# Two bit-linear stages: one normalised tile of four moves to ACT, and the high part is written from unscaled data

## The chip, the cores and the metric

The program runs on one NeuronCore of a Trainium2 chip. The metric is device time of one execution in microseconds, from runs on the chip; of the kernel before there are three, and one more execution that was profiled. Engines are called by the profile's names: PE (matmul), DVE (vector), ACT (activations), POOL, and SP, which only issues transfers here. SBUF and PSUM are the core's memories, PSUM being the one that PE writes.

## The reference

The program is a chain of six residual stages over x of shape 4 x 1024 x 256 (4096 rows): a binarised feed-forward layer, local attention, the feed-forward layer again, a bit-linear layer, attention with relative positions, and the bit-linear layer again. Only the two bit-linear layers matter here. Each gets the layer-normalised x and adds half its result to x:

```
def _L1_ffn_ref(x, weight, ln_gamma, ln_beta):
    LN_EPS = 0.001; EPS = 1e-05; QB = 128.0
    mu = jnp.mean(x, axis=-1, keepdims=True)
    var = jnp.var(x, axis=-1, keepdims=True)
    xn = (x - mu) * jax.lax.rsqrt(var + LN_EPS) * ln_gamma + ln_beta
    beta = jnp.mean(jnp.abs(weight))
    w_q = jnp.clip(ste_round(weight / (beta + EPS)), -1.0, 1.0)
    gamma = jnp.max(jnp.abs(xn))
    xq = jnp.clip(xn * QB / gamma, -QB + EPS, QB - EPS)
    y = jnp.einsum('bsd,du->bsu', xq, w_q)
    return y * (gamma * beta / QB)
...
    x = x + 0.5 * _L1_ffn_ref(x, weight, gamma, beta)
```

`gamma` is one number for all 4096 x 256 values, so the largest value must be known before any row is scaled: that cuts the layer in two halves. `xq` is not rounded, so the matmul needs more than one f16 factor's precision.

## The kernel before, in words

x stays in SBUF as `G.x`, 32 tiles of 128 rows x 256 columns. Mean and variance per row are in `G.mv`, left there by the stage before. A chunk is CT = 4 tiles (512 rows); there are NC = 8 chunks. `bit_phase` is called twice, as stage 4 (`b0_` tiles, from 855 us in the profile) and as stage 6, the last (`b1_` tiles, from 2221 us, where the results are also stored). The profile shows both under `b_`.

Each engine runs its own list of instructions in order, written out by hand; semaphores (`s[...]`) order the engines among each other. A `wait_ge` holds everything behind it on its engine.

First half, per chunk i:
- DVE normalises four tiles into `xn` (line 1181), which has two buffers, so from chunk 2 on it waits for the transposes of chunk i-2. Then it takes the largest absolute value of chunk i-1 (`largest`, line 1173). After chunks 1 and 3 it also does parts of the quantisation of the weight.
- PE transposes the chunk's tiles into PSUM `psT`, in two halves k of 128 features (line 1251).
- ACT multiplies by the layer's gain and adds its offset, PSUM to `xT` in SBUF (line 1129), once for each k.

Then DVE and POOL find the global maximum, and DVE writes `gi` (128 over the maximum, line 1195).

Second half, per chunk i:
- ACT scales `xT` in place by `gi` (line 1134), DVE clips it in place (`clip`, line 1199), ACT copies it to f16 as `xhi` (line 1139), DVE writes the f16 rest as `xlo` (`low_part`, line 1206).
- PE multiplies both parts by the ternary weight, 16 matmuls into `psY` (line 1262), and raises `Y`.
- DVE adds the result times `osc` to x (`residual`, line 1212). In stage 4 it also takes the moments for the next stage (lines 1220 and 1226); in stage 6 SP stores the chunk.

`xhi`, `xlo` and `psY` have two buffers each: the high and low parts of chunk i wait for `Y` of chunk i-2. ACT's list is scale 0, scale 1, high 0, scale 2, high 1, scale 3, (wait for Y 0) high 2, and so on. DVE's list is clip 0, clip 1, low 0, clip 2, low 1, residual 0, clip 3, low 2, residual 1, and so on, with aggregate and moments beside the residual in stage 4.

Of the kernel before, what the change touches and what calls it, by code (L numbers as in the profile page):

```python
# [7 lines left out]
ALU = mybir.AluOpType  # L8
ACT = mybir.ActivationFunctionType
AX = mybir.AxisListType  # L10
P = 128
B, S, D = 4, 1024, 256
NT = B * S // P
TPB = S // P
KD = D // P
HID = 1024
MH = HID // P
CT = 4
NC = NT // CT
# [13 lines left out]
def step(eng, ins, c):  # L33

    ins.then_inc(c.sem, 1)
    c.k += 1
    eng.wait_ge(c.sem, c.value())


def sems(nc, G, prefix, names):  # L40

    s = {n: nc.alloc_semaphore(f"{prefix}_{n}") for n in names.split()}
    G.live.extend(s.values())
    return s
# [1014 lines left out]
def bit_phase(nc, G, A, r, out=None):  # L1059
# [3 lines left out]
    with ExitStack() as ctx:  # L1063
        sb = lambda n, sh, d=F32: ctx.enter_context(nc.sbuf_tensor(f"b{r}_{n}", sh, d))
# [6 lines left out]
        eps = sb("eps", [P, 2])  # L1071
        sd = sb("sd", [P, NT])
        rstd = sb("rstd", [P, NT])
        var = sb("var", [P, NT])
        sd2 = sb("sd2", [P, NT])
        scl = sb("scl", [P, NT])
        wsum = sb("wsum", [P, 1])
        wall = sb("wall", [P, 1])
        thr = sb("thr", [P, 2])
        tmax = sb("tmax", [P, NC])  # L1080
        pmax = sb("pmax", [P, 1])
        gall = sb("gall", [P, 1])
        gi = sb("gi", [P, 1])
        osc = sb("osc", [P, 1])
        xn = sb("xn", [P, 2, CT, D])
        xT = sb("xT", [P, NC, KD, CW])
        xhi = sb("xhi", [P, 2, KD, CW], F16)
# [1 line left out]
        sums = sb("sums", [P, CT, 6])  # L1089
        psT = ps("psT", [P, 2, KD, 512])  # L1090
        psY = ps("psY", [P, 2, CT, D])
        s = sems(nc, G, f"bit{r}", "w_in gb_in eps sd norm var sd2 scl wsum wall quant xn xT xTev tmax max1 gmax gdve "
                 "scaled xq xhi xlo Y out sums stat stored")
        block = ctx.enter_context(nc.Block())

        @block.sync
        def _(sp):
            with nc.allow_non_contiguous_dma("gamma and beta by feature, once"):
                sp.dma_start(gm[:, :], A["gamma"].rearrange("(k p) -> p k", p=P)).then_inc(s["gb_in"], 16)
                sp.dma_start(bt[:, :], A["beta"].rearrange("(k p) -> p k", p=P)).then_inc(s["gb_in"], 16)  # L1100
            sp.dma_start(w[:, :, :], A["weight"].rearrange("(k p) d -> p k d", p=P)).then_inc(s["w_in"], 16)
            clear_old(G, sp)
            sp.wait_ge(s["gb_in"], 32)
            if last_phase:
                rows = out.rearrange("b (t p) d -> p (b t) d", p=P)
                for i in range(NC):
                    sp.wait_ge(s["out"], i + 1)
                    sp.dma_start(rows[:, i * CT:(i + 1) * CT, :],
                                 G.x[:, i * CT:(i + 1) * CT, :]).then_inc(s["stored"], 16)
                sp.wait_ge(s["stored"], 16 * NC)  # L1110
# [8 lines left out]
        @block.scalar  # L1119
        def _(act):  # L1120
            act.wait_ge(s["eps"], 1)
            nc.scalar.activation(sd[:, :], G.mv[:, :, 1], ACT.Sqrt, bias=eps[:, 0:1]).then_inc(s["sd"], 1)  # L1122
            act.wait_ge(s["var"], 1)
            nc.scalar.activation(sd2[:, :], var[:, :], ACT.Sqrt, bias=eps[:, 1:2]).then_inc(s["sd2"], 1)  # L1124
            act.wait_ge(s["gb_in"], 32)
            for i in range(NC):
                for k in range(KD):
                    act.wait_ge(s["xT"], i * KD + k + 1)
                    nc.scalar.activation(xT[:, i, k, :], psT[:, i % 2, k, :], ACT.Identity, bias=bt[:, k:k + 1],
                                         scale=gm[:, k:k + 1]).then_inc(s["xTev"], 1)  # L1130
            act.wait_ge(s["gdve"], 4)
            for i in range(NC + 1):
                if i < NC:
                    nc.scalar.activation(xT[:, i, :, :], xT[:, i, :, :], ACT.Copy, scale=gi[:, :]).then_inc(s["scaled"], 1)  # L1134
                if i >= 1:
                    act.wait_ge(s["xq"], i)
                    if i >= 3:
                        act.wait_ge(s["Y"], i - 2)
                    nc.scalar.activation(xhi[:, (i - 1) % 2, :, :], xT[:, i - 1, :, :], ACT.Copy).then_inc(s["xhi"], 1)  # L1139

        @block.vector
        def _(dve):
# [3 lines left out]
            norm = Count(s["norm"])  # L1146
# [4 lines left out]
            scale = Count(s["scl"])  # L1151
            step(dve, nc.vector.reciprocal(scl[:, :], sd2[:, :]), scale)  # L1152
            step(dve, nc.vector.tensor_tensor(scl[:, :], scl[:, :], rstd[:, :], ALU.mult), scale)

            quant = Count(s["quant"])

            def quantise(part):
                if part == 0:
                    dve.wait_ge(s["w_in"], 16)
                    nc.vector.tensor_reduce(wsum[:, :], w[:, :, :], AX.XY, ALU.add,  # L1160
                                            apply_absolute_value=True).then_inc(s["wsum"], 1)
                if part == 1:
                    dve.wait_ge(s["wall"], 1)
                    step(dve, nc.vector.tensor_scalar(wall[:, :], wall[:, :], 1.0 / (D * D), None, ALU.mult), quant)
                    step(dve, nc.vector.tensor_scalar(thr[:, 0:1], wall[:, :], 1e-5, 0.5, ALU.add, ALU.mult), quant)
                    step(dve, nc.vector.tensor_scalar(thr[:, 1:2], thr[:, 0:1], -1.0, None, ALU.mult), quant)
                    step(dve, nc.vector.tensor_scalar(wt[:, :, :], w[:, :, :], thr[:, 1:2], None, ALU.is_lt), quant)
                    nc.vector.scalar_tensor_tensor(wq[:, :, :], w[:, :, :], thr[:, 0:1], wt[:, :, :], ALU.is_gt,
                                                   ALU.subtract).then_inc(s["quant"], 1)

            def largest(i):
                dve.wait_ge(s["xTev"], i * KD + KD)
                nc.vector.tensor_reduce(tmax[:, i:i + 1], xT[:, i, :, :], AX.XY, ALU.max,
                                        apply_absolute_value=True).then_inc(s["tmax"], 1)

            for i in range(NC):
                if i >= 2:
                    dve.wait_ge(s["xT"], (i - 1) * KD)
                for t in range(CT):
                    g = i * CT + t  # L1180
                    nc.vector.tensor_scalar(xn[:, i % 2, t, :], G.x[:, g, :], G.mv[:, g, 0:1], scl[:, g:g + 1],  # L1181
                                            ALU.subtract, ALU.mult).then_inc(s["xn"], 1)
                if i in (1, 3):
                    quantise(i // 2)
                if i >= 1:
                    largest(i - 1)
# [4 lines left out]
            g = Count(s["gdve"])  # L1191
# [8 lines left out]
                                        ALU.max).then_inc(s["xq"], 1)  # L1200

            def low_part(i):
                dve.wait_ge(s["xhi"], i + 1)
                if i >= 2:
                    dve.wait_ge(s["Y"], i - 1)
                nc.vector.tensor_tensor(xlo[:, i % 2, :, :], xT[:, i, :, :], xhi[:, i % 2, :, :],  # L1206
                                        ALU.subtract).then_inc(s["xlo"], 1)
# [35 lines left out]
        @block.tensor  # L1243
        def _(pe):
            for i in range(NC):
                pe.wait_ge(s["xn"], i * CT + CT)
                if i >= 2:
                    pe.wait_ge(s["xTev"], (i - 1) * KD)
                for k in range(KD):
                    for t in range(CT):  # L1250
                        last = nc.tensor.transpose(psT[:, i % 2, k, t * P:t * P + P], xn[:, i % 2, t, k * P:k * P + P],
                                                   G.ident[:, :])
                    last.then_inc(s["xT"], 1)
            pe.wait_ge(s["quant"], 5)
            for i in range(NC):
                pe.wait_ge(s["xlo"], i + 1)
                if i >= 2:
                    pe.wait_ge(s["out"], i - 1)
                for t in range(CT):
                    for k in range(KD):  # L1260
                        for part, x in enumerate((xhi, xlo)):
                            last = nc.tensor.matmul(psY[:, i % 2, t, :], x[:, i % 2, k, t * P:t * P + P], wq[:, k, :],  # L1262
                                                    start=(k + part == 0), stop=(k == KD - 1 and part == 1),
                                                    skip_group_check=True)
                last.then_inc(s["Y"], 1)
# [1279 lines left out]
```

## Time and profile before

| | us |
|---|---|
| median of 3 runs (lowest, highest) | 2291.6 (2290.39, 2296.07) |
| the profiled execution's own time | 2287.45 |
| its span, first to last instruction | 2285.7 |
| PE busy in the span | 2010.9 (88%) |
| DVE busy | 1642.6 (72%) |
| ACT busy | 1221.4 (53%) |
| POOL busy | 495.5 (22%) |
| TensorE clock granted, mean over the span | 0.936 |

Busy time is the time in which an engine was executing; register, branch, semaphore and transfer-issuing instructions are not counted. The shares are averages over six stages with different limits, so they say little of one stage. The clock is a share of TensorE's full 2.4 GHz; 0.50 is its other level, 1.2 GHz. Start times count from the start of the span. The last 5.6 us of the span, after the last residual, are the last store.

### The profile page before, as it was taken

The numbers are of one execution on the slowest core, as the hardware profiler recorded it, in microseconds if no ns is written. First come the engines' busy times: TensorE is split into PE (matmuls) and PEld (weight loads), VectorE is DVE, ScalarE is ACT, GpSimd is POOL, SyncE is SP. The second block draws the span as 40 slices with busy tenths as digits, with TensorE's granted clock in tenths as the row PEclk, the third lists the DMA queues.
The fourth block names the chain that finished last, engine by engine and source line by source line (L and its number), as shares of the span: only waits on it lengthen the run. The fifth ranks groups of instructions, "written<-read, shape, count | busy, mean of one in ns | idle before, by whom it ended". The sixth has DMA issues, their size and how long they took to land. (4 is left out here: it accounts for less than half of the span.)

```text
span 2285.7 us, 74481 instructions
## 1 busy us (share of the span) xinstructions
PE 2010.9 (88%) x32248; PEld 1276.1 (56%) x32248; DVE 1642.6 (72%) x2668; ACT 1221.4 (53%) x1870; POOL 495.5 (22%) x804
## 2 busy tenths in 40 slices
PE   3996999999987985798878999999999999999985
PEld 2663565656655654457854555555555555555543
DVE  6776555554546778776676888888888888888847
ACT  3772232313234765223315777777776777777754
POOL 0003000000000000000014544345443544435410
PEclk8998898999999996899967999999999999999997
DMA  3001000000000000342485544545544555455312
GB/s 113 1 1 28 21 2 20 3 20 3 1 21 1 1 1 5 103 144 97 190 294 139 144 128 129 133 127 140 132 128 127 145 142 133 115 138 138 101 29 74
DMA packets 273791, 195.11 MB, mean 85 GB/s; under 512 B 206744, under 2 KB 260310, under 8 KB 273210
## 3 DMA queue, kind: packets, MB, share of 16 engines
q1 hardware_dynamic: 262586, 139.27, 23.9%
q0 software_dynamic: 10496, 50.75, 5.9%
q8 instruction: 256, 4.19, 0.8%
q14 instruction: 69, 0.57, 0.1%
q10 hardware_dynamic: 384, 0.33, 0.0%
HBM read 91.69 MB, written 93.88 MB: 81 GB/s over the span
## 5 line engine op out<-in xcount | busy, mean ns | idle before, releaser
L2158 DVE TENSOR_REDUCE a1c_nm<-a1c_S 128x1 f32<-128x1024 f32 x512 | 609.6, 1218 | 83.6 <-PE a1c_S L2245 83.1
L2092 ACT ACTIVATE a1c_PT<-a1c_ST 128x1024 f32<-128x1024 f32 x499 | 509.8, 1022 | 67.0 <-PE a1c_ST L2245 64.3
L2109 ACT ACTIVATE a1c_Pb<-a1c_S,a1c_nm 128x192 f32<-128x192 f32 (+1 forms) x512 | 212.2, 415 | 202.5 <-DVE a1c_nm L2158 201.2
L2031 POOL TENSOR_TENSOR a1c_lt<-a1c_lt 128x256 f32<-128x256 f32 (+5 forms) x448 | 254.0, 567 | 35.5
L2148 DVE COPY a1c_PbT<-a1c_T 96x512 f32<-96x512 f32 x256 | 175.8, 687 | 98.5 <-PE a1c_T L2277 96.1
L2245 PE MATMUL a1c_ST<-a1c_Q,a1c_KR 57*128 57x256 f16 (+2 forms) x1066 | 176.5, 286 | 29.6 <-ACT a1c_PT L2092 19.3
L2245 PE MATMUL a1c_S<-a1c_KL,a1c_Q 54*32 54x512 f16 (+11 forms) x3136 | 193.7, 327 | 0.3
L2245 PE MATMUL a1c_S<-a1c_KR,a1c_Q 54*32 54x512 f16 (+13 forms) x2816 | 182.0, 317 | 12.8 <-DMA a1c_Gx<-a_bias 10.2
L2245 PE MATMUL a1c_S<-a1c_Gx,ident 64*32 64x96 f32 (+2 forms) x4352 | 186.1, 242 | 0.0
L2023 POOL DMA_DIRECT2D a_band<-a1c_Pb x128 | 71.0, 555 | 494.7 <-ACT a1c_Pb L2109 494.6
L2277 PE MATMUL a1c_T<-ident,a1c_Pb 128*96 128x128 f32 x1024 | 169.5, 289 | 0.8 <-DVE a1c_mhl L2172 0.8
L2245 PE MATMUL a1c_ST<-a1c_Q,a1c_KL 57*128 57x128 f16 (+1 forms) x932 | 150.0, 266 | 17.5 <-ACT a1c_PT L2092 16.8
L596 ACT ACTIVATE a_PT<-a_R 128x1024 f32<-128x1024 f32 x80 | 77.5, 1021 | 144.4 <-PE a_R L956 94.2
L1115 POOL PARTITION_ALL_REDUCE b_wall<-b_wsum x2 | 0.8, 404 | 704.4 <-DVE b_wsum L1160 704.4
L2277 PEld LDWEIGHTS a1c_T<-ident,a1c_Pb 128*96 128x96 f32 x1024 | 102.7, 129 | 88.8 <-issue 55.7
L312 DVE TENSOR_TENSOR f_hlo<-f_h,f_hhi 128x512 f16<-128x512 f32 x128 | 88.0, 687 | 69.1 <-ACT f_hhi L230 69.0
L2245 PEld LDWEIGHTS a1c_S<-a1c_Gx,ident 64*32 64x32 f32 x4352 | 126.4, 110 | 14.0 <-issue 0.7
L225 ACT ACTIVATE f_h<-f_psH,b,a 128x512 f32<-128x512 f32 x128 | 99.3, 776 | 59.8 <-PE f_psH L336 58.3
L2245 PE MATMUL a1c_PV<-a1c_PT,a1c_VU 128*17 128x512 f32 (+3 forms) x1280 | 127.5, 470 | 0.0
L2245 PE MATMUL a1c_PV<-a1c_PT,a1c_VL 128*17 128x512 f32 (+3 forms) x1280 | 127.4, 470 | 0.0
L655 DVE TENSOR_REDUCE a_mx<-a_R 128x8 f32<-128x1024 f32 x64 | 75.4, 1221 | 66.8 <-PE a_R L878 66.8
L347 PE MATMUL f_psY<-sw2T,f_hhi 128*128 128x256 f16 x512 | 118.6, 273 | 1.0 <-DVE f_hlo L312 1.0
(366 smaller groups left out, 4096.4 us busy)
## 6 DMA issues: line engine op xcount, KB each, us to landing
a_band<-a1c_Pb POOLq DMA_DIRECT2D x128, 384.0 KB, 3.4
a_bias<-a1b_G SPq DMA_DIRECT2D x32, 768.0 KB, 9.3
a1c_Gx<-a_bias SPq DMA_DIRECT2D x128, 192.0 KB, 4.4
a1c_Dt<-a_band SPq DMA_DIRECT2D x128, 126.0 KB, 3.7
a1c_Q<-a_qk SPq DMA_DIRECT2D x192, 64.0 KB
a1c_Vw<-a_values SPq DMA_DIRECT2D x64, 102.0 KB, 3.0
a1c_KL<-a_qk SPq DMA_DIRECT2D x96, 64.0 KB
a1c_KR<-a_qk SPq DMA_DIRECT2D x90, 64.0 KB
```

What stands on the lines that cost most here:

```text
L225: nc.scalar.activation(h[:, n % NB, :], psH[:, n % NB, :], ACT.Gelu, bias=G.b1[:, m:m + 1], scale=G.a1[:, m:m + 1]).then_inc(s["h"], 1)
L312: nc.vector.tensor_tensor(hlo[:, n % NB, :], h[:, n % NB, :], hhi[:, n % NB, :], ALU.subtract).then_inc(s["hlo"], 1)
L347: last = nc.tensor.matmul(psY[:, i % 2, t, :], x[:, n % NB, t * P:t * P + P], G.sw2T[:, m, :], start=(m + part + t % 2 == 0), stop=(m == M ...
L596: nc.scalar.activation(PT[:, n % 2, 2 * a:2 * a + 2, :], R[:, 2 * a:2 * a + 2, :], ACT.Exp, scale=0.25).then_inc(s["sexp"], 1)
L655: nc.vector.tensor_reduce(dst[:, 2 * a:2 * a + 2], src[:, 2 * a:2 * a + 2], AX.X, ALU.max, negate=True).then_inc(s["smax"], 1)
L2031: add = lambda o, x, y: nc.gpsimd.tensor_tensor(o, x, y, ALU.add)
L2092: nc.scalar.activation(PT[:, q % 8, :, :], place(q), ACT.Exp).then_inc(s["exp"], 1)
L2109: nc.scalar.activation(Pb[:, band_slot(I, c), w0:w1], SP[:, t % 2, I * P - 32 + w0:I * P - 32 + w1], ACT.Exp, bias=nm[:, t // 16 % 2, col: ...
L2148: nc.vector.tensor_copy(PbT[:, e % RING, :], T[0:BW, :]).then_inc(s["Tb_ev"], 1)
L2158: nc.vector.tensor_reduce(nm[:, t // 16 % 2, col:col + 1], SP[:, t % 2, :], AX.X, ALU.max, negate=True).then_inc(s["max"], 1)
L2245: return nc.tensor.matmul(out, w, x, start=start, stop=stop, skip_group_check=True)
L2277: ins = nc.tensor.transpose(T[0:BW, at:at + P], Pb[:, band_slot(I, c), BW * ch:BW * ch + BW], G.ident[:, :])
```

## The change

In the first half DVE normalises three tiles of a chunk and ACT the fourth, as `scl * x + off`, with a new small tile `off` = -mean * `scl` that DVE computes once per stage. ACT does this for chunk i+1 ahead of its affine instructions of chunk i. PE waits for both engines.

In the second half ACT writes `xhi` straight from the unscaled `xT` with the scale `gi`, and only then scales `xT` in place; it waits for its own high part before that. ACT's list becomes high 0, scale 0, high 1, scale 1, (wait for Y 0) high 2, scale 2, (wait for Y 1) high 3, scale 3, and so on. DVE's clip still waits for the scale and its list keeps its order; the low part now waits for the clip instead of the high part. The high part is thus that of the unclipped value, and the low part is the clipped value less it.

```diff
--- before.py
+++ after.py
@@ -1074,6 +1074,7 @@
         var = sb("var", [P, NT])
         sd2 = sb("sd2", [P, NT])
         scl = sb("scl", [P, NT])
+        off = sb("off", [P, NT])
         wsum = sb("wsum", [P, 1])
         wall = sb("wall", [P, 1])
         thr = sb("thr", [P, 2])
@@ -1089,7 +1090,7 @@
         sums = sb("sums", [P, CT, 6])
         psT = ps("psT", [P, 2, KD, 512])
         psY = ps("psY", [P, 2, CT, D])
-        s = sems(nc, G, f"bit{r}", "w_in gb_in eps sd norm var sd2 scl wsum wall quant xn xT xTev tmax max1 gmax gdve "
+        s = sems(nc, G, f"bit{r}", "w_in gb_in eps sd norm var sd2 scl wsum wall quant xn xna xT xTev tmax max1 gmax gdve "
                  "scaled xq xhi xlo Y out sums stat stored")
         block = ctx.enter_context(nc.Block())
 
@@ -1122,21 +1123,30 @@
             nc.scalar.activation(sd[:, :], G.mv[:, :, 1], ACT.Sqrt, bias=eps[:, 0:1]).then_inc(s["sd"], 1)
             act.wait_ge(s["var"], 1)
             nc.scalar.activation(sd2[:, :], var[:, :], ACT.Sqrt, bias=eps[:, 1:2]).then_inc(s["sd2"], 1)
+            def normalise(i):
+                g = i * CT + CT - 1
+                if i >= 2:
+                    act.wait_ge(s["xT"], (i - 1) * KD)
+                nc.scalar.activation(xn[:, i % 2, CT - 1, :], G.x[:, g, :], ACT.Identity, bias=off[:, g:g + 1],
+                                     scale=scl[:, g:g + 1]).then_inc(s["xna"], 1)
+
             act.wait_ge(s["gb_in"], 32)
+            act.wait_ge(s["scl"], 3)
+            normalise(0)
             for i in range(NC):
+                if i + 1 < NC:
+                    normalise(i + 1)
                 for k in range(KD):
                     act.wait_ge(s["xT"], i * KD + k + 1)
                     nc.scalar.activation(xT[:, i, k, :], psT[:, i % 2, k, :], ACT.Identity, bias=bt[:, k:k + 1],
                                          scale=gm[:, k:k + 1]).then_inc(s["xTev"], 1)
             act.wait_ge(s["gdve"], 4)
-            for i in range(NC + 1):
-                if i < NC:
-                    nc.scalar.activation(xT[:, i, :, :], xT[:, i, :, :], ACT.Copy, scale=gi[:, :]).then_inc(s["scaled"], 1)
-                if i >= 1:
-                    act.wait_ge(s["xq"], i)
-                    if i >= 3:
-                        act.wait_ge(s["Y"], i - 2)
-                    nc.scalar.activation(xhi[:, (i - 1) % 2, :, :], xT[:, i - 1, :, :], ACT.Copy).then_inc(s["xhi"], 1)
+            for i in range(NC):
+                if i >= 2:
+                    act.wait_ge(s["Y"], i - 1)
+                nc.scalar.activation(xhi[:, i % 2, :, :], xT[:, i, :, :], ACT.Copy, scale=gi[:, :]).then_inc(s["xhi"], 1)
+                act.wait_ge(s["xhi"], i + 1)
+                nc.scalar.activation(xT[:, i, :, :], xT[:, i, :, :], ACT.Copy, scale=gi[:, :]).then_inc(s["scaled"], 1)
 
         @block.vector
         def _(dve):
@@ -1151,6 +1161,7 @@
             scale = Count(s["scl"])
             step(dve, nc.vector.reciprocal(scl[:, :], sd2[:, :]), scale)
             step(dve, nc.vector.tensor_tensor(scl[:, :], scl[:, :], rstd[:, :], ALU.mult), scale)
+            step(dve, nc.vector.scalar_tensor_tensor(off[:, :], G.mv[:, :, 0], -1.0, scl[:, :], ALU.mult, ALU.mult), scale)
 
             quant = Count(s["quant"])
 
@@ -1176,7 +1187,7 @@
             for i in range(NC):
                 if i >= 2:
                     dve.wait_ge(s["xT"], (i - 1) * KD)
-                for t in range(CT):
+                for t in range(CT - 1):
                     g = i * CT + t
                     nc.vector.tensor_scalar(xn[:, i % 2, t, :], G.x[:, g, :], G.mv[:, g, 0:1], scl[:, g:g + 1],
                                             ALU.subtract, ALU.mult).then_inc(s["xn"], 1)
@@ -1200,7 +1211,7 @@
                                         ALU.max).then_inc(s["xq"], 1)
 
             def low_part(i):
-                dve.wait_ge(s["xhi"], i + 1)
+                dve.wait_ge(s["xq"], i + 1)
                 if i >= 2:
                     dve.wait_ge(s["Y"], i - 1)
                 nc.vector.tensor_tensor(xlo[:, i % 2, :, :], xT[:, i, :, :], xhi[:, i % 2, :, :],
@@ -1243,7 +1254,8 @@
         @block.tensor
         def _(pe):
             for i in range(NC):
-                pe.wait_ge(s["xn"], i * CT + CT)
+                pe.wait_ge(s["xn"], (i + 1) * (CT - 1))
+                pe.wait_ge(s["xna"], i + 1)
                 if i >= 2:
                     pe.wait_ge(s["xTev"], (i - 1) * KD)
                 for k in range(KD):
```

## Rows read from the trace of the kernel before

**Rows 1.** Last stage's second half: us; busy PE, PEld, DVE, ACT, POOL; PEclk, DMA, GB/s

```profile
2251.60:2280.20 28.60, 17.32 (x128) 13.03 (x128) 23.98 (x24) 16.65 (x16) 0.00 (x0) 0.84 0.37 125
```

**Rows 2.** Chain of waits, last stage: start us, us, what

```profile
2262.70 1.28 DVE x L1212
2263.97 0.60 DVE b_xT L1199
...
2265.63 1.28 DVE x L1212
```

**Rows 3.** Timeline of DVE, last stage's first half: start us, us, what, [idle before]

```profile
2224.68 0.19 DVE L1153 TENSOR_TENSOR b_scl<-b_scl,b_rstd 128x32 f32<-128x32 f32 x1
2224.91 2.67 DVE L1181 TENSOR_SCALAR b_xn<-x,mv,b_scl 128x256 f32<-128x256 f32 x8
...
2238.17 1.22 DVE L1173 TENSOR_REDUCE b_tmax<-b_xT 128x1 f32<-128x1024 f32 x1
...
2241.13 1.22 DVE L1173 TENSOR_REDUCE b_tmax<-b_xT 128x1 f32<-128x1024 f32 x1 [0.46 <-ACT b_xT L1129]
...
2248.92 1.22 DVE L1173 TENSOR_REDUCE b_tmax<-b_xT 128x1 f32<-128x1024 f32 x1 [1.20 <-ACT b_xT L1129]
```

**Rows 4.** Timelines of PE and ACT, last stage's first half, chunk 4

```profile
2238.31 1.97 PE L1251 MATMUL b_psT<-ident,b_xn 128*128 128x128 f32 x8 [2.20 <-DVE b_xn L1181]
...
2239.46 1.63 ACT L1129 ACTIVATE b_xT<-b_psT,b_bt,b_gm 128x512 f32<-128x512 f32 x2 [2.54 <-PE b_psT L1251]
```

**Rows 5.** ACT's groups, shapes apart: line, names, shapes, count, busy us, mean ns

```profile
L2109 ACT ACTIVATE a1c_Pb<-a1c_S,a1c_nm 128x192 f32<-128x192 f32 x384 | 161.8, 421 | 156.4 <-DVE a1c_nm L2158 155.2
...
L1134 ACT ACTIVATE b_xT<-b_xT,b_gi 128x1024 f32<-128x1024 f32 x16 | 18.0, 1134 | 5.4 <-DVE b_gi L1195 5.4
L1139 ACT ACTIVATE b_xhi<-b_xT 128x1024 f16<-128x1024 f32 x16 | 16.8, 1053 | 18.6 <-PE b_psY L1262 11.7 <-DVE b_xT L1199 6.8
```

**Rows 6.** Timeline of ACT, last stage's second half

```profile
2251.61 2.19 ACT L1134 ACTIVATE b_xT<-b_xT,b_gi 128x1024 f32<-128x1024 f32 x2 [2.72 <-DVE b_gi L1195]
...
2259.82 1.06 ACT L1139 ACTIVATE b_xhi<-b_xT 128x1024 f16<-128x1024 f32 x1 [2.05 <-PE b_psY L1262]
...
2264.85 1.06 ACT L1139 ACTIVATE b_xhi<-b_xT 128x1024 f16<-128x1024 f32 x1 [0.71 <-PE b_psY L1262]
```

**Rows 7.** Timeline of DVE, last stage's second half

```profile
2254.78 1.22 DVE L1206 TENSOR_TENSOR b_xlo<-b_xT,b_xhi 128x1024 f16<-128x1024 f32 x1 [0.25 <-ACT b_xhi L1139]
...
2261.56 1.22 DVE L1206 TENSOR_TENSOR b_xlo<-b_xT,b_xhi 128x1024 f16<-128x1024 f32 x1
...
2273.28 1.22 DVE L1206 TENSOR_TENSOR b_xlo<-b_xT,b_xhi 128x1024 f16<-128x1024 f32 x1
```

**Rows 8.** Timeline of ACT in a feed-forward stage, an instruction and its dependent

```profile
745.14 0.77 ACT L225 ACTIVATE f_h<-f_psH,b,a 128x512 f32<-128x512 f32 x1
745.94 0.63 ACT L230 ACTIVATE f_hhi<-f_h 128x512 f16<-128x512 f32 x1
```

**Rows 9.** Timeline of PE, last stage's second half

```profile
2256.15 0.37 PE L1262 MATMUL b_psY<-b_wq,b_xhi 128*128 128x256 f16 x1 [8.07 <-DVE b_xlo L1206]
...
2262.84 0.28 PE L1262 MATMUL b_psY<-b_wq,b_xhi 128*128 128x256 f16 x1 [0.89 <-DVE b_xlo L1206]
```

**Rows 10.** PE's busy time and granted clock in two stretches: us, busy (count), PEclk

```profile
902.10:908.90 6.80, 4.74 (x22) 0.50 0.00 0
2256.10:2260.40 4.30, 4.25 (x21) 0.50 0.01 4
```

**Rows 11.** Timeline of DVE, first stage's second half

```profile
888.52 1.23 DVE L1206 TENSOR_TENSOR b_xlo<-b_xT,b_xhi 128x1024 f16<-128x1024 f32 x1 [0.25 <-ACT b_xhi L1139]
...
908.53 1.22 DVE L1206 TENSOR_TENSOR b_xlo<-b_xT,b_xhi 128x1024 f16<-128x1024 f32 x1
...
913.03 1.22 DVE L1206 TENSOR_TENSOR b_xlo<-b_xT,b_xhi 128x1024 f16<-128x1024 f32 x1
...
921.24 1.25 DVE L1212 SCALAR_TENSOR_TENSOR x<-b_psY,b_osc,x 128x1024 f32<-128x1024 f32 x1
```

## The prediction

> **What bounds the kernel now.** The edit touches only the two bit-linear stages, so I read their stretches first, then the chain of waits inside the second, then the timelines of DVE, ACT and PE. Each stage has a first half (normalise, transpose, affine, largest value) and a second (scale, clip, split in high and low part, matmul, residual). The second half of the last stage takes 28.6 us, with PE busy for 17.3 of them at a mean granted clock of 0.84, DVE for 24.0 and ACT for 16.7 [rows 1]. There the chain goes through DVE alone, one chunk every 2.93 us (2262.70 to 2265.63): residual, clip, low part [rows 2]. The reader should see which instructions run ahead. Before the edit ACT's scaling of a chunk stands ahead of the high part that waits for a free buffer, so DVE's clip always finds scaled data, and PE, with one chunk of slack, starts as soon as the low part is there.
>
> **First half, part by part.** Added: one 128x32 DVE instruction (`off`); its neighbour of that shape is at 2224.68 and the next starts at 2224.91, so +0.23 us [rows 3]. Removed: one normalising instruction of four per chunk on DVE; eight take 2.67 us, a step of 0.32 us each (2.67 less one of 0.41, by 7) [rows 3]. Not every one is on the path. Take T(i), the end of DVE's normalising of chunk i. PE starts 0.14 us after it, the second ACT affine is over 2.92 us after it, and DVE's reduction begins at T+2.96 (T(4) 2238.17, reduction 2241.13) [rows 3, 4]. DVE's order is normalise i+1, reduce i, so where that latency is last, T(i+2) = T(i) + 2.96 + 1.13 (reduction, step) + 1.29, two chunks in 5.38 us; after, 1.29 becomes 0.97 and two chunks take 5.06. Followed through the half, the path is: normalise 0, latency, reduce 0, normalise 2, reduce 1, normalise 3, (weight) reduce 2, normalise 4, reduce 3, normalise 5, latency, reduce 5, normalise 7, latency, reduce 7. It holds the normalising of six chunks; that of 1 and 6 lies beside a latency. So the last reduction, now 2248.92, comes 6 x 0.32 - 0.23 = 1.7 us earlier per stage, 3.4 us in all, if PE's clock is as before.
>
> What ACT takes on, a 128x256 Identity with two pointer operands, has no row. It is above the 0.42 us of 192 columns with one pointer and below the 1.13 us of 1024 columns [rows 5]; I take 0.56, near the first. Beside the 1.63 us of a pair of affines [rows 4] that is 2.2 us in a chunk of 2.5, and it is issued before the affines of the chunk before, while ACT waits for PE. So I hide it. Without the cover it lengthens the 2.96 by 0.56, two chunks take 5.6 instead of 5.38, and the first half gains nothing: 0 to -3.4 us for both stages.
>
> **Second half, start.** Before: scale 0, scale 1, high part 0; clip 0, clip 1, low part 0 starts at 2254.78 [rows 6, 7]. After, ACT does high 0, scale 0, high 1, scale 1, and clip 1 is still ahead of low part 0 on DVE. The high part now reads with a pointer scale and writes f16: the row without scale is 1.05, the one with scale and an f32 write 1.13 [rows 5]; I take 1.13 (the lower end would take 1 us off the final sum). A wait on ACT's own last result costs 0.03 us more than the 0.77 of the instruction (745.14 to 745.94) [rows 8]. From 2251.61: high 0 to 2252.74, scale 0 from 2252.77 to 2253.90, high 1 (overlapping by 0.09, as the two scales do in 2.19) to 2254.94, scale 1 to 2256.10, clip 1 from 2256.14, low part 0 at 2256.73. That is 1.95 us later per stage.
>
> **Second half, the loop.** This is the term that decides. High part i waits for Y(i-2), the matmuls that used its buffer. That wait was on the high part alone; now scale i is queued behind it on ACT, clip i waits for scale i, and low part i-1 stands behind clip i on DVE, though its data is long ready. Y(i-1) waits for low part i-1. So Y(i-2) -> high i -> scale i -> clip i -> low i-1 -> Y(i-1): a ring with no slack, one turn per chunk. Its price at the low clock:
>
> - low part start to PE start 1.28 (2261.56 to 2262.84) [rows 7, 9]
> - PE start to ACT released 3.67 (2256.15 to 2259.82) [rows 6, 9]
> - high part 1.13, own wait 0.03, scale 1.13, to DVE 0.04
> - clip to low part 0.60 [rows 2]
>
> Sum 7.88 us. At the high clock the PE term is 2.01 (2262.84 to 2264.85) [rows 6, 9], and the turn 6.22. DVE's other work (low part 1.14, residual 1.2 and, in the first stage only, moments and aggregate, some 1.6, as its chunks are 4.49 apart, 908.53 to 913.03 [rows 11], and the last stage's 2.93) takes 2.3 to 3.9 us beside the 7.2 before the next clip: hidden.
>
> Which clock? A burst of 16 matmuls now comes after 7.88 - 3.6, some 4.3 us of PE idleness. Traces of before: PE began at 0.50 and held it for 4.3 us of unbroken work [rows 10], more than the 3.6 of a burst; in the first stage, with chunks 4.49 apart and some 2 us of matmuls in each, the clock fell to 0.50 from 902.10 to 908.90 [rows 10]. I take the low clock for all turns. The Trainium skill, "TensorE: Matmul & The Clock Gate", section "HAM oscillation — how this bites in real kernels", tells of a kernel whose bursts, shorter than the waits between them, each start at the low rate; by it the sum is the 7.88 turn, and by a clock that stays up it is the 6.22 turn. No stretch of this trace has just this pattern.
>
> The low parts 0 to 6 are six turns apart; low part 7 has no clip ahead of it and is off the ring.
> Last stage: 2256.73 + 6 x 7.88 = 2304.0 against 2273.28 [rows 7], +30.7. Its tail is 32 matmuls nearly unbroken, which ran high before. A matmul costs 0.104 more at the low clock (3.67 less 2.01, by 16). If the clock rises after 4.3 us as above, 20 of them (0.21 each) are low: +2.1, or +3.3 if it stays low.
> First stage: 888.52 + 1.95 + 47.3 = 937.8 against 913.03 [rows 11], +24.7; less than in the last stage, since a chunk took 4.49 there already. Tail: low part 7 follows low part 6 by DVE's 3.9 us above, and Y(7) ends 1.28 + 3.67 later, at +8.85, for a residual that started at +8.21 (921.24) [rows 11]: +0.6.
>
> **Sum.** 30.7 + 2.1 + 24.7 + 0.6 - 3.4 = +54.7 us on a span of 2285.7, an execution of 2287.45. The median of the runs is 2291.6, 4.15 above; the difference carries over: 2346.3, and I write 2345, since a few bursts may see the clock rise near their end. Other stages run the same code and cost nothing; a shift of the clock's timing in them may give or take 3 us.
>
> **Rivals.**
> 1. *The clock stays up in the ring.* Turns of 6.22: the last stage 2294.1 against 2273.3, +20.8, the first 927.8 against 913.0, +14.8; with -3.4, +32: 2324. For: the last stage had a mean of 0.84 [rows 1] though PE paused in every chunk. Against: its share of work there was 2.01 of 2.93; here it would be 2.01 of 6.22, with over 4 us of pause in every turn.
> 2. *ACT's normalising sits in the chain of the first half.* The gain of 3.4 is gone, with the ring as forecast: 2349. For: it is issued ahead of the affines; against: ACT idles before them.
> 3. *The ring does not close, so not slower.* If the buffer wait of high part 2 were met when ACT gets there (2256.1), ACT would stay ahead with 2.2 us a chunk under DVE's 2.93, and the stage would stay DVE's. Then only the start counts, 2 x 1.95 - 3.4 = +0.5: 2292, and 2288 if the late start falls into DVE's idleness before residual 0. It decides on whether Y(0) ends before ACT's third high part. Against: Y(0) cannot start before low part 0 at 2256.73, so ACT must wait; this needs DVE to run low part 1 past the waiting clip 2. The chain shows clip ahead of low part each time [rows 2], in program order. The Trainium skill, the same page, section "Architectural detail: the array is 16× 32×32, not 1× 128×128", says in my words that ACT and DVE serve their queues strictly in order; by it the sum is 2345, and with passing allowed it would be 2292. The trace agrees so far as it shows clips and low parts in the order issued.
>
> **How the numbers follow.** Forecast 0.77 (2345), rival 1 0.10 (2324), rival 2 0.09 (2349), rival 3 0.04 (2292 or 2288). The range, 2323 to 2354: below it takes in the high clock throughout, above the lost gain, a low tail (+1.2) and 3 us of clock shift elsewhere; rival 3 is left out. What this kernel can tell from no change is 0.3%, 7 us: faster 0.01, same 0.03, slower 0.96.
>
> **What would show it.** Second halves: ACT's idleness before every high part from the third on, released by PE, and DVE's idleness before each clip, released by ACT's scale; steps of 7.9 (or 6.2) us between low parts, equal in both stages; PEclk near 0.5. First halves: reductions 0.32 us closer per pair of chunks, the last 1.7 us earlier from the start of the stage. Wrong if DVE shows no idleness before the clips, if low parts stay 2.93 us apart, or if ACT's Identity is what ends DVE's or PE's waits in the first half.

## The result, and the profile after

The changed kernel takes 2343.55 us (median of 4 runs, 2342.47 to 2346.78), the kernel before 2293.75 (4 runs, 2290.39 to 2296.07): a ratio of 1.0221, 95% interval 1.0201 to 1.0240. Slower by 2.2%. The profiled execution took 2342.7 us, its span is 2341.0, 55.3 longer than before's.

The first view is the busy time by stretch of the changed kernel: last stage's first half, its second half, first stage's second half (columns as in [rows 1]).

```profile
2246.03:2274.50 28.47, 12.57 (x64) 10.42 (x64) 21.78 (x51) 17.73 (x28) 0.77 (x2) 0.72 0.04 10
2274.50:2335.80 61.30, 27.74 (x128) 17.91 (x128) 24.35 (x24) 18.24 (x16) 0.00 (x0) 0.60 0.18 60
884.99:950.50 65.51, 27.90 (x128) 17.71 (x128) 37.19 (x88) 18.24 (x16) 0.00 (x0) 0.60 0.00 0
```

The second half of the last stage lasts 61.3 us where it lasted 28.6 [rows 1]. DVE is busy for the same 24 us and ACT for 18.2 instead of 16.7. PE, with the same 128 matmuls, is busy for 27.7 us instead of 17.3, at a mean clock of 0.60 instead of 0.84. No engine is busy for even half of the stretch; each waits for another in turn.

The chain of waits of the last stage, one turn (it answers to [rows 2]):

```profile
2308.01 1.16 ACT b_xhi L1147
...
2309.19 1.16 ACT b_xT L1149
...
2310.37 0.04 DVE b_xT L1210
2310.40 0.57 issue
2310.97 1.23 DVE b_xlo L1217
...
2312.25 3.61 PE b_psY L1274 x16
2315.86 0.02 issue
2315.88 1.16 ACT b_xhi L1147
```

Before, one chunk was three DVE entries in a row. Now the chain goes round: ACT's high part, ACT's scale, DVE's clip, DVE's low part, PE's 16 matmuls, and ACT's next high part 7.87 us after the last (2308.01 to 2315.88). DVE's timeline, to set beside [rows 7]:

```profile
2279.68 1.22 DVE L1217 TENSOR_TENSOR b_xlo<-b_xT,b_xhi 128x1024 f16<-128x1024 f32 x1
...
2310.37 0.69 DVE L1210 TENSOR_SCALAR b_xT<-b_xT 128x1024 f32<-128x1024 f32 x1 [4.85 <-ACT b_xT L1149]
2310.97 1.22 DVE L1217 TENSOR_TENSOR b_xlo<-b_xT,b_xhi 128x1024 f16<-128x1024 f32 x1
2312.11 1.28 DVE L1223 SCALAR_TENSOR_TENSOR x<-b_psY,b_osc,x 128x1024 f32<-128x1024 f32 x1
2318.24 0.69 DVE L1210 TENSOR_SCALAR b_xT<-b_xT 128x1024 f32<-128x1024 f32 x1 [4.86 <-ACT b_xT L1149]
...
2326.72 1.22 DVE L1217 TENSOR_TENSOR b_xlo<-b_xT,b_xhi 128x1024 f16<-128x1024 f32 x1
...
2334.52 1.28 DVE L1223 SCALAR_TENSOR_TENSOR x<-b_psY,b_osc,x 128x1024 f32<-128x1024 f32 x1 [1.61 <-PE b_psY L1274]
```

In the last stage DVE sat idle for 4.57 to 4.86 us before each clip from the fourth on (6.12 before the third, which has no residual ahead of it), released by ACT's scale (line 1149), and the low part that PE needs stands right behind. In the first stage, where moments and aggregates lie in between, 3.27 to 3.40 us were left from the fifth clip on. ACT's side, beside [rows 6]:

```profile
2274.50 1.15 ACT L1147 ACTIVATE b_xhi<-b_xT,b_gi 128x1024 f16<-128x1024 f32 x1 [2.72 <-DVE b_gi L1206]
2275.68 1.15 ACT L1149 ACTIVATE b_xT<-b_xT,b_gi 128x1024 f32<-128x1024 f32 x1
...
2315.88 1.15 ACT L1147 ACTIVATE b_xhi<-b_xT,b_gi 128x1024 f16<-128x1024 f32 x1 [5.55 <-PE b_psY L1274]
2317.06 1.15 ACT L1149 ACTIVATE b_xT<-b_xT,b_gi 128x1024 f32<-128x1024 f32 x1
```

Every high part from the third on waits for PE, over 5 us, and the scale follows 0.03 us after it. In PE's rows the first of two stretches is a burst, the second most of the 4.28 us of pause behind it (us, busy and count, clock, DMA share, GB/s), as in [rows 10]:

```profile
2312.20:2315.90 3.70, 3.60 (x16) 0.50 0.42 141
2315.90:2320.10 4.20, 0.00 (x0) 0.50 0.00 0
```

One burst of 16 in each stage was shorter, because the clock rose before its end; in the last stage this one, where the others took 3.6 us at 0.50 to 0.52:

```profile
2296.78:2300.09 3.31, 3.31 (x16) 0.56 0.37 126
```

The first half did get shorter. DVE's timeline, beside [rows 3]; from `off` to the last reduction:

```profile
2249.62 0.19 DVE L1164 SCALAR_TENSOR_TENSOR b_off<-mv,b_scl 128x32 f32<-128x32 f32 x1
2249.85 2.03 DVE L1192 TENSOR_SCALAR b_xn<-x,mv,b_scl 128x256 f32<-128x256 f32 x6
...
2271.81 1.22 DVE L1184 TENSOR_REDUCE b_tmax<-b_xT 128x1 f32<-128x1024 f32 x1 [1.52 <-ACT b_xT L1141]
```

The normalising starts at 2249.85 and the last reduction at 2271.81, 21.96 us; before it was 2224.91 to 2248.92, 24.01 us. ACT's groups, beside [rows 5]:

```profile
L1149 ACT ACTIVATE b_xT<-b_xT,b_gi 128x1024 f32<-128x1024 f32 x16 | 18.4, 1147 | 0.5
L1147 ACT ACTIVATE b_xhi<-b_xT,b_gi 128x1024 f16<-128x1024 f32 x16 | 18.3, 1145 | 71.7 <-PE b_psY L1274 66.3 <-DVE b_gi L1206 5.4
...
L1130 ACT ACTIVATE b_xn<-x,b_off,b_scl 128x256 f32<-128x256 f32 x16 | 9.3, 590 | 2.0 <-DVE b_off L1164 2.0
```

The table splits each profiled span. A first half goes from the start of ACT's table load to the end of the write of `gi`, a second half from there to the end of the last aggregate (first stage) or residual (last stage); each is the difference of rows of DVE's and ACT's timelines. The rest is the span less the four: the same code in every kernel here.

| profiled run | first stage: first, second half | last stage: first, second half | rest | median, ratio to before (95%) |
|---|---|---|---|---|
| before | 30.2, 40.8 | 30.3, 28.5 | 2155.9 | |
| changed | 28.5, 65.5 | 28.4, 61.3 | 2157.2 | 2343.55, 1.0221 (1.0201 to 1.0240) |
| four high-part buffers | 28.4, 42.8 | 28.5, 30.6 | 2154.1 | 2289.33, 1.0011 (0.9999 to 1.0023) |
| low part ahead of clip | 28.5, 45.8 | 28.6, 37.1 | 2152.9 | 2299.72, 1.0052 (1.0036 to 1.0067) |
| first-half edit alone | 28.6, 40.8 | 28.5, 28.3 | 2153.7 | 2284.3, 0.9989 (0.9980 to 0.9999) |
| second-half edit alone | 30.2, 65.2 | 30.3, 61.6 | 2161.7 | 2346.33, 1.0254 (1.0236 to 1.0272) |
| extra matmuls in the ring | 28.6, 57.3 | 28.6, 53.1 | 2159.8 | 2322.12, 1.0144 (1.0130 to 1.0158) |
| both cuts of the ring | 28.6, 41.2 | 28.5, 28.5 | 2157.6 | 2287.4, 0.9990 (0.9981 to 0.9999) |
| changed, high part doubled | 28.6, 73.5 | 28.6, 68.6 | 2160.9 | 2359.75, 1.0302 (1.0289 to 1.0315) |
| before, high part doubled | 30.3, 42.1 | 30.3, 29.8 | 2157.9 | 2292.43, 1.0015 (1.0004 to 1.0025) |
| first-half edit, PE warm for the second | 28.4, 39.1 | 28.6, 26.8 | 2157.9 | 2283.38, 0.9966 (0.9953 to 0.9978) |
| the same, PE warm in both | 27.3, 39.1 | 26.7, 28.3 | 2156.8 | 2281.91, 0.9971 (0.9960 to 0.9983) |
| the same, warmed for longer | 28.0, 39.1 | 27.7, 26.8 | 2161.3 | 2281.28, 0.9961 (0.9946 to 0.9976) |

The four halves went from 129.8 to 183.8 us, +54.0 of the 55.3. The rest varies by 9 us from one profiled run to another with the same code, so an edit of 2 us is to be read in the halves, not in one span. The kernel before took 2287.3 to 2289.8 us (medians) beside the experiments, less than beside the change, so totals are compared as ratios. One of the 12 runs of "both cuts of the ring" took 6247 us, the others 2285 to 2291; why is open, and its ratio is without that run.

### The profile page after: what moved, and what is told of

The parts are those of the page before. It is cut to its first block and busy times, and to the rows that moved or that the text cites. A ratio compares the mean times of both kernels' runs of the same rounds, so it can differ in the third digit from the quotient of the medians.

```text
span 2341.0 us, 74477 instructions
## 1 busy us (share of the span) xinstructions
PE 2026.6 (87%) x32248; PEld 1282.1 (55%) x32248; DVE 1638.4 (70%) x2654; ACT 1232.4 (53%) x1886; POOL 495.1 (21%) x804
## 5 line engine op out<-in xcount | busy, mean ns | idle before, releaser
L2257 PE MATMUL a1c_ST<-a1c_Q,a1c_KR 57*128 57x256 f16 (+2 forms) x1066 | 176.3, 285 | 30.2 <-ACT a1c_PT L2104 19.6
L2257 PE MATMUL a1c_ST<-a1c_Q,a1c_KL 57*128 57x128 f16 (+1 forms) x932 | 149.9, 266 | 18.4 <-ACT a1c_PT L2104 16.8
```

The lines of the kernel that those rows point to most:

```text
L2257: return nc.tensor.matmul(out, w, x, start=start, stop=stop, skip_group_check=True)
```

## The experiments

**The ring cut at its buffer.** `xhi` has four buffers; the low part and the matmuls read it by the new index (not shown), and nothing else changes.

```diff
-        xhi = sb("xhi", [P, 2, KD, CW], F16)
+        xhi = sb("xhi", [P, 4, KD, CW], F16)
...
-                if i >= 2:
-                    act.wait_ge(s["Y"], i - 1)
-                nc.scalar.activation(xhi[:, i % 2, :, :], xT[:, i, :, :], ...
+                if i >= 4:
+                    act.wait_ge(s["Y"], i - 3)
+                nc.scalar.activation(xhi[:, i % 4, :, :], xT[:, i, :, :], ...
```

> The changed kernel with four high-part buffers instead of two, so high part i waits for the matmuls of chunk i-4; order of both engines' lists unchanged. Ring theory (matmuls i-2, high i, scale i, clip i, low i-1, matmuls i-1): with two more chunks of slack at the buffer wait the ring no longer sets the pace, low parts go back to 2.93 us apart in the last stage and 4.49 in the first, DVE never idles long before a clip after the second one. Only the later start of low part 0 (some 1.9 us per stage) and the first half's gain (1.8 per stage) stay: 2292 to 2296 us, within 3 us of the kernel before. Rival (the second half is slow because ACT's two instructions per chunk are longer and wait on each other, or because PE fell to its low clock of itself): stays at 2335 to 2344.

DVE's low parts 0, 2, 3 and 6 of the last stage (`gi` was written at 2248.72):

```profile
2253.95 1.22 DVE L1217 TENSOR_TENSOR b_xlo<-b_xT,b_xhi 128x1024 f16<-128x1024 f32 x1
...
2260.72 1.22 DVE L1217 TENSOR_TENSOR b_xlo<-b_xT,b_xhi 128x1024 f16<-128x1024 f32 x1
...
2263.65 1.22 DVE L1217 TENSOR_TENSOR b_xlo<-b_xT,b_xhi 128x1024 f16<-128x1024 f32 x1
...
2272.44 1.22 DVE L1217 TENSOR_TENSOR b_xlo<-b_xT,b_xhi 128x1024 f16<-128x1024 f32 x1
```

From the third on they are 2.93 us apart, as before, and the first is 5.23 us after `gi` instead of 3.20. The two second halves gave back 53.5 of the 57.5 us that they had cost, with the longer ACT instructions, their order and the wait between them in place. They keep 2.0 us each over before: the late start alone. The ratio, 1.0011, is at the upper end of what was expected: 2296 us beside a before of 2293.75 is 1.0010.

**The ring cut at DVE's order.** Two buffers, but the low part ahead of the clip.

```diff
             for i in range(NC + 4):
-                if i < NC:
-                    clip(i)
                 if 1 <= i <= NC:
                     low_part(i - 1)
+                if i < NC:
+                    clip(i)
```

> The changed kernel with two buffers as it is, but in DVE's list low part i-1 stands ahead of clip i. Ring theory: the edge from clip i to low part i-1 is cut, the ring that is left runs from matmuls i-2 to high i, scale i, clip i, low i, matmuls i and so covers two chunks: 1.28 + 2.01 to 3.67 + 2.33 + 0.60 and one residual of 1.2 between clip and low part, 7.4 to 9.1 us for two chunks, 3.7 to 4.6 a chunk in the last stage; in the first, with moments and aggregate in it, 4.5 to 5.3. Total 2295 us, between 2288 and 2305. If DVE's order is not part of it (ACT's queue behind the buffer wait alone makes the pace): stays at 2340 or above.

Low parts 2, 3, 4, 5 and 6 of the last stage:

```profile
2262.91 1.21 DVE L1217 TENSOR_TENSOR b_xlo<-b_xT,b_xhi 128x1024 f16<-128x1024 f32 x1
...
2265.84 1.21 DVE L1217 TENSOR_TENSOR b_xlo<-b_xT,b_xhi 128x1024 f16<-128x1024 f32 x1
...
2271.73 1.21 DVE L1217 TENSOR_TENSOR b_xlo<-b_xT,b_xhi 128x1024 f16<-128x1024 f32 x1
...
2274.66 1.21 DVE L1217 TENSOR_TENSOR b_xlo<-b_xT,b_xhi 128x1024 f16<-128x1024 f32 x1
...
2279.92 1.21 DVE L1217 TENSOR_TENSOR b_xlo<-b_xT,b_xhi 128x1024 f16<-128x1024 f32 x1
```

They come in pairs: 2.93, 5.89, 2.93, 5.26, two chunks in 8.8 and 8.2 us, as a ring over two chunks has it. So DVE's order, which the change did not touch, is part of the ring: with the two calls swapped the second halves gave back 44 of the 57.5 us. The total is at the upper end of what was expected, not at its middle: 2295 us was meant beside a before of 2293.75, a ratio of 1.0005, its upper end of 2305 is 1.0049, and 1.0052 (1.0036 to 1.0067) was measured. PE's clock changed its level inside the last stage's bursts here. The pair for the first two low parts shown began low and ended high (us, busy and count, clock, DMA share, GB/s):

```profile
2264.18:2266.50 2.32, 2.32 (x12) 0.50 0.59 201
2266.50:2269.30 2.80, 2.77 (x22) 0.89 0.56 187
```

Less the 5.41 us of its other terms (1.28 + 2.33 + 0.60 + 1.2), the two turns of 8.82 and 8.19 us leave 3.4 and 2.8 for PE, between 2.01 and 3.67. So the mechanism held, and the 2295 us had the low clock's share too small.

**Each half of the change by itself.** The kernel before with the first-half part of the diff alone, and the kernel before with the second-half part alone (the second-half part is ACT's loop behind `act.wait_ge(s["gdve"], 4)` and the wait in `low_part`; the rest of the diff is the first-half part).

> The kernel before with the first-half edit alone (ACT normalises one tile of four); its second half untouched. My theory: the traces' first halves are 1.8 and 1.7 us shorter, so 3.5 us under the kernel before, a ratio of 0.9985: just below or at what 5 rounds can tell. Rival (the gain came from another phase of PE's clock, and ACT's part costs as much as it saves): no difference, or 1 us slower.

> The kernel before with the second-half edit alone. If the two edits are independent: the changed kernel's time plus the 3.5 us of the first half, 2347 us, and low parts 7.88 us apart. Rival (the first half leaves PE's clock or the engines in a state that makes the second half's cost): under 2340.

The first halves are 28.6 and 28.5 us against 30.2 and 30.3, the total 3.0 us less (ratio 0.9989): the gain of the first half is there without the other edit. The second-half edit costs 2.5% alone, its halves 65.2 and 61.6 us as in the changed kernel. The four halves are 3.5 us above the changed kernel's, just the first half's gain; the ratio, 1.0254 against 1.0221, says more, but its interval overlaps and the rest was long in the profiled run. The two edits add up, and all of the loss is the second's.

**The clock inside the ring.** 24 matmuls that nobody waits for, behind each chunk's 16 but the last; PE also waits for the last transposes' results to be read, since the extra ones write over them.

```diff
             pe.wait_ge(s["quant"], 5)
+            pe.wait_ge(s["xTev"], NC * KD)
...
                 last.then_inc(s["Y"], 1)
+                if i < NC - 1:
+                    for _ in range(24):
+                        nc.tensor.matmul(psT[:, 0, 0, 0:D], wq[:, 0, 0:P], wq[:, 0, :], start=True, stop=True,
+                                         skip_group_check=True)
```

> The changed kernel with 24 extra matmuls (128x256, f16, into the unused transposes' PSUM, their result used by nobody) behind each chunk's 16, except the last. They fill PE's pause inside the ring and wait for nothing. Ring theory with the low clock as a term of it: if they keep the clock at its high level, a chunk's matmuls take 2.01 instead of 3.67 us and the turn 6.22 instead of 7.88; 12 turns, some 20 us less than the changed kernel: 2321 to 2326 us, though PE has more work. If the clock is no cost here: 2343 or more. If the clock stays low in spite of them, 40 matmuls take 8.5 us, over the turn's 7.88: about 2352.

Low parts 2 and 3 on DVE:

```profile
2288.46 1.22 DVE L1217 TENSOR_TENSOR b_xlo<-b_xT,b_xhi 128x1024 f16<-128x1024 f32 x1
...
2294.66 1.22 DVE L1217 TENSOR_TENSOR b_xlo<-b_xT,b_xhi 128x1024 f16<-128x1024 f32 x1
```

PE's extra matmuls between those two, and the first matmul of the next burst; then the clock of the half's first burst and of the third, each with its extra matmuls:

```profile
2291.49 2.78 PE L1281 MATMUL b_psT<-b_wq 128*128 128x256 f16 x24
2295.94 0.28 PE L1275 MATMUL b_psY<-b_wq,b_xhi 128*128 128x256 f16 x1 [1.66 <-DVE b_xlo L1217]
...
2275.68:2282.29 6.61, 6.61 (x40) 0.67 0.00 0
2289.74:2294.27 4.53, 4.53 (x40) 1.00 0.34 116
```

The turn is 6.20 us (2288.46 to 2294.66) where the prediction's rival had 6.22. The extra 24 take 2.78 us of the pause, every burst but the first of each half runs at the high level, and the kernel with 296 instead of 128 matmuls in this half is 0.8% faster than the changed one (1.0144 by 1.0221). The first burst of each half still starts low, so the first of its six turns stays at 7.94 and 7.95 us: ten turns are shorter, not the twelve expected, and the halves fell by 16.5 us, not some 20. So of the 7.87 us of a turn 1.67 is PE's clock, a consequence of the pauses that the ring itself makes; the other 6.2 is the ring.

**The same microsecond in the ring and outside it.** Each high part is also written to a spare tile.

```diff
+                nc.scalar.activation(spare[:, i, :, :], xT[:, i, :, :], ACT.Copy, scale=gi[:, :])
                 nc.scalar.activation(xhi[:, i % 2, :, :], xT[:, i, :, :], ACT.Copy, scale=gi[:, :]).then_inc(s["xhi"], 1)
```

> The changed kernel with each high part written twice, first into a spare tile nobody reads; the added instruction is a step of 1.05 us on ACT behind the buffer wait. Ring theory: it is paid in full at each turn and twice at the start, 1.05 x (6 + 2) per stage, 16.8 us in all: 2360 us, low parts 8.9 us apart. Rival (ACT has slack, as its 36% share of the second half says, and something else sets the pace): under 2348.

> The kernel before with the same instruction doubled in the same way. There it lies beside DVE: ACT's chunk becomes about 3.0 us against DVE's 2.93 (last stage) and 4.49 (first), and the start of low part 0 is 1 us later per stage. Ring theory (no ring in this order): +2 to +4 us over the kernel before, a quarter or less of what the same instruction costs in the changed kernel. Rival (ACT's work in the second half costs the same in either order): +13 or more.

In the changed kernel low parts 4 and 5 are now 8.92 us apart, 1.05 more:

```profile
2329.02 1.22 DVE L1219 TENSOR_TENSOR b_xlo<-b_xT,b_xhi 128x1024 f16<-128x1024 f32 x1
...
2337.94 1.22 DVE L1219 TENSOR_TENSOR b_xlo<-b_xT,b_xhi 128x1024 f16<-128x1024 f32 x1
```

Its second halves grew by 8.0 and 7.3 us, 15.2 together against 16.8 expected; by the ratios (1.0302 and 1.0221) the total grew by 0.8%, some 18 us. In the kernel before the same instruction (there without a scale) cost 1.3 us a half, 0.95 of it the later first low part (4.15 us after `gi` instead of 3.20). The same work costs six times as much where the ring passes through it; ACT's busy share says nothing of that.

**Both cuts together**, four buffers and the low part first:

> The changed kernel with four high-part buffers and low part i-1 ahead of clip i, a candidate for the best. Ring theory: nothing of the ring is left, and low part 0 starts right behind clip 0, at or ahead of where it started before. First half -1.8 and -1.7 us, second halves DVE's 2.93 and 4.49 a chunk: 2288 to 2291 us, 3 to 5 under the kernel before. Rival (ACT's high part ahead of its scale costs at every clip): 2293 or more.

Second halves of 41.2 and 28.5 us, within 0.4 of those before the change, and 0.9990 in all: the change without its ring keeps its first half's gain and no more, some 2 us where 3 to 5 were expected.

**Toward a better kernel.** The first-half edit alone (0.9989) was as good as any so far, and the clock had proved to be worth 1.67 us a burst. PE's first burst of the second half comes after 8.07 us of pause [rows 9] and runs at the low level [rows 10], and DVE then waits for it. So, on top of the first-half edit:

```diff
             pe.wait_ge(s["quant"], 5)
+            pe.wait_ge(s["xTev"], NC * KD)
+            for _ in range(36):
+                nc.tensor.matmul(psT[:, 0, 0, 0:D], wq[:, 0, 0:P], wq[:, 0, :], start=True, stop=True,
+                                 skip_group_check=True)
```

> The kernel before with the first-half edit alone, and 36 extra matmuls on PE (128x256, f16, result unused) between its last transposes and the first matmuls of the second half, while DVE and POOL find the global maximum. If the clock goes up behind some 4.3 us of them (20 at 0.21 us), the other 16 take 1.7 us and PE is done before low part 0, which starts 3.2 us after gi: the first burst takes 2.01 instead of 3.67 us, residual 0 comes 1.66 us earlier, and DVE sets the pace from there: -1.6 us per stage, 3.3 us under the first-half edit alone, 0.3% under the kernel before. If the first burst's clock is hidden beside DVE: no difference from the first-half edit alone. If the clock stays low, 36 take 7.7 us and may hold up the first burst by a microsecond: +2.

DVE's low parts 0 and 2 of the last stage (`gi` at 2248.86):

```profile
2252.07 1.23 DVE L1219 TENSOR_TENSOR b_xlo<-b_xT,b_xhi 128x1024 f16<-128x1024 f32 x1 [0.25 <-ACT b_xhi L1151]
...
2257.11 1.22 DVE L1219 TENSOR_TENSOR b_xlo<-b_xT,b_xhi 128x1024 f16<-128x1024 f32 x1
```

Low part 2 comes 8.25 us after `gi` instead of 9.73 in the run without (9.98 in the kernel before), the second halves are 1.7 and 1.5 us shorter, and the ratio is 0.9966 (0.9953 to 0.9978): 0.3% under the kernel before, as expected.

With 22 transposes ahead of chunk 0 and 6 behind each chunk's 8 as well:

> As the run with the warm second half, and in the first half too PE is kept at work: 22 extra 128x128 transposes into the unused PSUM of the matmuls before chunk 0 and 6 behind each chunk's 8. If the clock stays high, the latency from DVE's normalising to its reduction is 2.32 instead of 2.96 us, two chunks take 2.32 + 1.13 + 0.97 = 4.42 instead of 5.06 us: 1.5 to 2.5 us less per stage, 3 to 5 us under the run with the warm second half. If the first half is bound elsewhere: no difference. If the clock stays low, 14 transposes take 3.0 us a chunk, more than the 2.5 of a chunk: 3 to 4 us slower per stage.

The first halves fell by 1.1 and 1.9 us against the run without, where 1.5 to 2.5 were expected; the last stage's second half lost 1.5 again. So the total did not come 3 to 5 us lower, and its ratio can't be told from that run's. PE, bridging stretch and first burst there (us, busy and count, clock):

```profile
2241.50:2244.70 3.20, 2.66 (x26) 1.00 0.00 0
2244.80:2249.10 4.30, 1.45 (x14) 1.00 0.00 0
2249.20:2252.80 3.60, 3.60 (x18) 0.53 0.00 0
```

The 36 ran at the high level and were over in 4.09 us; in the 2.9 us of pause the clock was still high and it fell at the burst's start. With 58 in place of 36:

> As the run with both halves kept warm, with 58 extra matmuls instead of 36 between the halves. In that run's last stage the 36 were over in 4.09 us and PE then paused until its first burst of the second half at 2249.19, which fell to the low clock right at its start (0.53 in its first 3.6 us) and kept its cost of 1.6 us. 58 at 0.109 us fill 6.3 of the 7.0 us. If the pause is the cause, low part 2 comes 8.25 us after gi in both stages (it came 9.78 after it in the last), the last stage's second half is 26.8 us, and the total about 1.5 us under that run, 0.35 to 0.4% under the kernel before. If the clock falls anyway, no difference.

Low part 2 is back at 8.25 us after `gi`, the last stage's second half at 26.8. Its first halves, 28.0 and 27.7, gained less than in the run before, with the same code: the first eight transposes of the last stage took 1.80 us here and 1.10 there. Why the clock was late here is open. The ratio of 0.9961 (0.9946 to 0.9976) is the best measured, 0.4% under the kernel before; the three warm kernels can't be told apart by their intervals.

## Why the prediction was right

The forecast was 2345 us, the median 2343.55.

- *First half, -1.7 us a stage*: -1.7 and -1.8. `off` is a step of 0.23 us (2249.62 to 2249.85), the normalising on ACT 0.590 against the 0.56 taken, hidden as argued: rival 2 fell, the run with the first-half edit alone shows it.
- *Start of the second half, low part 0 1.95 us later*: 5.22 us after `gi` against 3.20, 2.0 later. The high part with a pointer scale and an f16 write takes 1.145 us, just above the upper bound of 1.134 from [rows 5].
- *The ring, 7.88 us a turn*: ten of the twelve turns took 7.87 to 7.95; one in each stage was shorter, 7.73 and 7.59. Six turns took 47.2 and 47.0 us against 47.3. That it is this ring, and that it closes through both the buffer and DVE's order, is what the two cuts show. Two of its terms were changed by experiment and counted in full at a turn, the high part (+1.05 us) and PE's burst (-1.67); the others are read from the chain. DVE's other work stayed hidden in both stages, as argued.
- *The clock*: low at the start of every burst in the ring, as forecast; in the two short turns it rose before the burst's end (3.46 us at 0.54 and 3.31 at 0.56), for which the forecast had allowed. The last stage's mean is 0.60 rather than "near 0.5", chiefly since in three of its six pauses the clock was up (0.85 to 0.90), where it is worth nothing: the burst behind each began at 0.50. Rival 1 gives the turn that the run with extra matmuls then measured. The Trainium skill, "TensorE: Matmul & The Clock Gate", section "HAM oscillation — how this bites in real kernels", tells of bursts shorter than the waits between them that each start at the low rate. The trace agrees: bursts of 3.6 us at 0.50, 4.28 us apart.
- *Tails*: +2.2 in the last stage against +2.1; nothing in the first against +0.6.
- *Sum*: +54.7 forecast, +54.0 in the four halves, +55.3 on the span. Rival 3 was wrong in just the point it named: ACT waited 5.62 us for `Y` at its third high part. The Trainium skill, "TensorE: Matmul & The Clock Gate", section "Architectural detail: the array is 16× 32×32, not 1× 128×128", says that ACT and DVE serve their queues strictly in order. The trace agrees: the ready low part never passed the waiting clip in DVE's rows.

That the forecast time lies within 1.5 us of the median is partly luck. Its starting point, 2291.6, was the median of three runs; with the fourth run that of the kernel before is 2293.75, and medians differ by 49.8 us where the halves differ by 54.0. The forecast also carried over 4.15 us between the profiled execution and the median; the changed kernel's profiled execution lies only 0.85 below its median. The shift of the rest, +1.3 us, is within the 9 us by which it varies, so no run tells it apart from nothing.

## What to carry to other kernels

Before moving work on an engine, write down the orders of both engines and walk from a buffer's release back to that release: if the walk comes home within one chunk, its length is the pace, whatever the busy shares say. A wait moved ahead of an instruction is a wait moved ahead of everyone who waits for that instruction, here DVE's clip and the ready low part behind it. Two more buffers were worth 53 us here, and two calls swapped in one list 44.

## What the runs showed of the hardware

An engine's pauses can raise the price of its own work: with a pause of 4.28 us in each turn ACT's high part came 3.63 us after the first of PE's 16 matmuls (2312.25 to 2315.88), and with 24 unused matmuls in that pause 1.95 us after it (2289.74 to 2291.69), so that more work ended sooner by 0.8%. A pause of 2.94 us behind 36 matmuls at the high level came three times: twice the next burst stayed high, once (the rows with 0.53 above) the clock fell at its start. With 58 matmuls and a pause of 0.54 us it stayed high both times.
